# Feed-forward layers one slot sooner in a slot-scheduled post-norm transformer layer

## What is computed

```python
x = layernorm(x + attention(x))        # 16 query heads of width 16, 4 key/value heads
gate, up = split(x @ Wgu_q.T)          # weights made ternary in groups of 64
h = silu(gate) * up                    # 1024 wide
x = layernorm(x + rms_norm(h) @ Wproj_q.T)
```

## Time and profile before

| | |
|---|---|
| median of 3 runs | 559.68 us (559.02 to 562.63) |
| the profiled execution | 559.17 us |
| its span | 557.2 us |
| work outside the span (559.17 - 557.2) | 1.97 us |
| one element in the middle of the run | about 29.6 us |

### The profile page before, as it was taken

How to read it: one execution, slowest core, us unless ns; L and a number is a source line. 1 busy time by engine, 2 the same in 40 slices (tenths; PEclk the granted TensorE clock), 3 DMA queues, 4 the chain that set the end, 5 groups by cost and what they waited for, 6 DMA issues and landing times. The chain is left out here.

```text
span 557.2 us, 13565 instructions
## 1 busy us (share of the span) xinstructions
PE 521.8 (94%) x4152; PEld 444.7 (80%) x4152; DVE 443.0 (80%) x1009; ACT 363.6 (65%) x735; POOL 332.5 (60%) x511
## 2 busy tenths in 40 slices
PE   4687999999999999999999999999999999999884
PEld 4677778788888888888888888888888888776773
DVE  6877796868888887878797878888898888875784
ACT  4553774657576767676777767676777676767553
POOL 4566774245665756575756656656657565656744
PEclk9896999999999999999999999999999999999997
DMA  9777173616253636354454536162627162010001
GB/s 233 133 153 121 45 138 74 115 58 115 51 107 57 131 55 135 69 124 79 106 98 95 105 83 117 65 119 57 121 41 164 16 152 51 22 41 1 19 21 38
DMA packets 83395, 49.16 MB, mean 88 GB/s; under 512 B 39696, under 2 KB 83344, under 8 KB 83344
## 3 DMA queue, kind: packets, MB, share of 16 engines
q1 hardware_dynamic: 81456, 47.87, 41.7%
q10 hardware_dynamic: 1888, 0.66, 0.5%
HBM read 33.29 MB, written 14.68 MB: 86 GB/s over the span
## 5 line engine op out<-in xcount | busy, mean ns | idle before, releaser
L867 DVE TENSOR_REDUCE row_max<-short_ps 128x2 f32<-128x512 f32 x256 | 169.8, 681 | 37.1 <-PE short_ps L579 35.7
L1055 POOL TENSOR_TENSOR h_lo<-h_f,h_hi 128x256 fp32r<-128x256 f32 x116 | 85.5, 737 | 163.9 <-ACT h_hi L766 163.7
L794 ACT ACTIVATE probs<-exp_ps 128x1024 f32<-128x1024 f32 x128 | 130.8, 1022 | 41.7 <-PE exp_ps L588 41.3
L579 PE MATMUL short_ps<-k_st,q_st 65*128 65x256 f32 x512 | 108.5, 296 | 3.8 <-DVE row_max L867 3.4
L775 ACT ACTIVATE tanh<-ffn_ps 128x256 f32<-128x256 f32 x120 | 45.9, 383 | 89.3 <-PE ffn_ps L607 89.3
L579 PEld LDWEIGHTS short_ps<-k_st,q_st 65*128 65x128 f32 x512 | 88.3, 193 | 15.2 <-issue 2.5
L1060 POOL TENSOR_TENSOR sq_sum<-sq_sum,h_sq 128x256 f32<-128x256 f32 x111 | 83.1, 749 | 7.0 <-ACT h_sq L830 6.7
L588 PE MATMUL exp_ps<-q_st,k_st 67*128 67x512 f32 x256 | 81.5, 400 | 3.4 <-DMA q_st<-shift_lo 3.2
L607 PE MATMUL ffn_ps<-x1T_hi,wguT 128*128 128x256 f32 x480 | 80.0, 289 | 3.7 <-DVE h_f L953 3.5
L620 PE MATMUL down_ps<-wpT,h_hi 128*128 128x256 f32 x256 | 79.4, 332 | 3.9 <-DVE h_lo L856 2.9
L607 PE MATMUL ffn_ps<-x1T_lo,wguT 128*128 128x256 f32 x480 | 77.9, 285 | 0.0
(11 more groups left out here) (110 smaller groups left out, 834.5 us busy)
## 6 DMA issues: line engine op xcount, KB each, us to landing
q_st<-q_dram SPq DMA_DIRECT2D x128, 128.0 KB, 3.9
q_dram<-q_p SPq DMA_DIRECT2D x16, 512.0 KB, 3.0
k_st<-k_dram SPq DMA_DIRECT2D x64, 64.0 KB, 2.4
res<-in_L_attn_x_dram SPq DMA_DIRECT2D x16, 256.0 KB, 2.8
xn<-in_L_attn_x_dram SPq DMA_DIRECT2D x62, 64.0 KB, 2.8
out_dram<-y_out SPq DMA_DIRECT2D x15, 256.0 KB, 2.9
wgu_raw<-in_L_ffn_w_gate_up_dram SPq DMA_DIRECT2D x8, 256.0 KB, 6.1
k_dram<-k_p SPq DMA_DIRECT2D x16, 128.0 KB, 2.5
```

Source lines behind the costliest of these rows:

```text
L579: last = pe.matmul(bank[:, t * S:(t + 1) * S], q_st[0:PAD, st.par, head, t * P:(t + 1) * P], k_st[0:PAD, st.par, st.s % 4, :], start=True, ...
L794: act.activation(probs[:, st.s % 4], exp_ps[:], ACT.Exp).then_inc(exp_done, 1)
L867: dve.tensor_reduce(row_max[:, st.par, head * TT:(head + 1) * TT], short(n, f"max{i}")[:].rearrange("p (t k) -> p t k", t=TT), AX.X, ALU.m ...
L1055: pool.tensor_tensor(h_p[1][:, st.s % 4, :], h_f[:, st.s % 2, :], h_p[0][:, st.s % 4, :].bitcast(F32), ALU.subtract).then_inc(h_lo, 1)
```

## The change

Nine offsets of the chain behind the attention fall by one: `LN1_APPLY`, `X1_T`, `X1_HIGH`, `X1_LOW`, `FFN0` with all its chunk steps, `DOWN0`, `Y_COPY`, and the sum of squares with its mean and root. The offsets of the output projection (26), `O_ADD` (26), `RSTD1` (27), `LN2_STATS` (42), `RSTD2`, `LN2_APPLY` and `STORE` stay. On POOL the four operations of `RSTD1` now stand ahead of the slot's `h_lo`. The banks of `sq`, `x1` and `shift0` change with the slots that they now fall in.

```diff
-LN1_APPLY = 28
-X1_T = 29
-FFN0 = 31
+LN1_APPLY = 27
+X1_T = 28
+FFN0 = 30
...
-BANK_TABLE = {0: {"max0": 2, "max1": 0, "sq": 1},
+BANK_TABLE = {0: {"max0": 2, "max1": 0},
...
-              4: {"max0": 0, "max1": 2, "k": 1},
-              5: {"max0": 2, "max1": 1, "shift0": 0, "x1": 2},
+              4: {"max0": 0, "max1": 2, "k": 1, "x1": 0},
+              5: {"max0": 2, "max1": 1, "shift0": 2},
...
-              7: {"max0": 2, "max1": 0, "v": 1}}
+              7: {"max0": 2, "max1": 0, "sq": 2, "v": 1}}
...
                         normalised(pool)
+                if st := n.once(RSTD1):
+                    wait(pool, var1_done, st.count(TT, TT))
...
                 if st := n.chunk(H_LOW0):
...
-                if st := n.once(RSTD1):
-                    wait(pool, var1_done, st.count(TT, TT))
...
```

More of the change, by code:

```diff
@@ L48 @@
 PROJ_O = 26
-LN1_APPLY = 28
-X1_T = 29
-FFN0 = 31
-DOWN0 = 33
-Y_COPY = 40
+LN1_APPLY = 27
+X1_T = 28
+FFN0 = 30
+DOWN0 = 32
+Y_COPY = 39
 TWO_BANKS = SLOTS * (B - 1) + EXP0 + SLOTS
-SUM_SQ = 40
+SUM_SQ = 39
 LN2_STATS = 42
@@ L65 @@
 RSTD1 = 27
[L66 to L73, removed]
+X1_HIGH = 28
+X1_LOW = 29
+GATE0 = 30
+H0 = 30
+H_HIGH0 = 31
+H_LOW0 = 31
+MEAN_SQ = 39
+INV = 39
 RSTD2 = 44
@@ L1050, in slot @@
                         normalised(pool)
+                if st := n.once(RSTD1):
+                    wait(pool, var1_done, st.count(TT, TT))
+                    pool.tensor_tensor(ve1[:], mv1[:, :, 1], ln_eps[:], ALU.add).then_inc(ve1_done, 1)
+                    wait(pool, ve1_done, st.count(1, 1))
+                    rsqrt(rstd1[:], ve1[:], rstd1_done)
+                    wait(pool, rstd1_done, st.count(1, 1))
+                    pool.tensor_tensor(mean1[:], mv1[:, :, 0], minus_one[:], ALU.mult).then_inc(mean1_done, 1)
+                    wait(pool, mean1_done, st.count(1, 1))
+                    pool.tensor_tensor(shift1[:], mean1[:], rstd1[:], ALU.mult).then_inc(shift1_done, 1)
                 if st := n.chunk(H_LOW0):
```

## The result

The changed kernel took 573.91 us (median of 4 runs, 573.10 to 575.31) against 559.70 for the kernel before (4 runs too). The ratio is 1.0246, interval 1.0205 to 1.0288: slower. The profiled execution took 575.31 us, its span is 573.5 (before: 557.2), 16.3 longer.

What follows compares the result with a forecast made beforehand. PE's own list was taken to set the 29.6 us element. Middle 0.56 x 13 = 7.3, head 1.5, tail 0: 8.8 us on 559.17 gives 568.0, plus 0.5 for the median: 568.5 us, range 563.5 to 572.5.

Steps and rivals of the forecast that it cites:

- Rival (a): PE's busy time hides slack, so the middle costs nothing and head and tail nearly cancel: 559.7 to 562; chance 0.16.
- Term 1: Slot 6: PE's low half newly waits for DVE's x1T_lo, 0.57 us an element (0.54 to 0.59).
- Term 2: Slot 7: the old wait for x1T_lo goes, giving back 0.09 us an element (0.06 to 0.13).
- Term 3: Slot 0: without the sum of squares, PE waits for h_f, 0.1 us an element on average (0 to 0.3).
- Number of elements: Middle of the run: the cost per element counts 13 times, for elements 1 to 13.
- Term 4: Head: slot 30 gets gate/up products that are not hidden, +1.5 us (0.8 to 2.0).
- Term 5: Tail: one slot fewer, but the last x1 is late and a tanh held back; 0 us (-1.5 to +1).
- The covers: Moved roots, x1, ms, bank users and the copy of down_ps are ready before their readers, so they cost nothing.

Runs made afterwards that it cites:

- low_first: Changed kernel with DVE's x1_low ahead of shift_rows in slot 5, so x1T_lo no longer waits for the turn of the maxima; 564.98 us, ratio 1.0087.
- low_later: Changed kernel with x1_low moved behind slot 5's second maximum, so the wait for x1T_lo gets longer; 580.37 us, ratio 1.0350.
- again: The changed kernel run once more without an edit; 570.63 us, ratio 1.0194.
- both: Changed kernel with the edits of low_first and sq_back together; 560.76 us, ratio 1.0002.
- sq_back: Changed kernel with only the sum of squares, its mean and root put back in slot 0; 569.67 us, ratio 1.0165.
- roots_back: Changed kernel with RSTD1's roots on POOL again behind h_lo and the sum of squares; 596.86 us, ratio 1.0644.
- roots_only: Kernel before the change with only RSTD1's four POOL operations moved ahead of the slot's h_lo; 562.34 us, ratio 1.0032.
- both_bout: Kernel of both, with ADD_BOUT (sum of residual and bias, POOL) in slot 7 instead of slot 0; 560.08 us, ratio 0.9992.

## Why the prediction was right and where it was wrong

**Direction and mechanism: right, and shown.** PE's list sets the period, and the new wait for `x1T_lo` is the largest loss: `low_first` takes it away and with it 0.65 of the 0.86. Rival (a), no difference, is dead: `low_later` shows that a longer wait comes back in the element one to one (0.593 for 0.60). The Trainium skill ("Perfetto Trace Analysis", "Identifying the Most-Contended Engine") advises to judge how close PE is to its roofline by weight load time and not by matmul busy time. By it there were 15% to spare here (25.55 of 29.99 us). That is room for a better list; it did not take up a new wait in this one, which came back in full.

**The size: wrong.** The forecast was 8.8 us and the range ended at 572.5; the first measurement gave 14.2 more (573.91 against 559.70), `again` 9.6 (570.63 against 561.02). The 570.63 lies inside the range, but by a start that happened to be early: the element missed in both. Behind the start, which is chance, the two profiles of the changed kernel are 13.2 and 12.9 us longer than that of the kernel before (16.3 - 3.1 and 568.7 - 557.2 + 1.4). By its own terms:

- **Term 1 (0.57): failed in one clause.** "After the wait, the chain low half, tanh, `gated`, `h_f`, next gate sets slot 6 as it did, so nothing is won back there." The wait itself is 0.53 on average, inside the bounds. But the chain is longer than it was: PE's first group after a stop takes 0.10 more, and `tanh` and `h_f` are as much later. 0.53 + 0.11 = 0.64; `low_first` gives 0.65. The prediction's own rows had it: the groups at 102.16 and 308.67, both behind a stop, are listed with 0.74, the one at 289.52 with 0.64.
- **Term 2 (-0.09): size right, place half wrong.** I had high to low half in slot 7 at 0.48; it is 0.56, since that high half itself comes out of the wait for `h_f` and is slow. 0.02 came back there, and 0.08 behind the low half, which no longer starts from a stop (3.35 to 3.27 in `both`).
- **Term 3 (0.08): failed, measured 0.30.** (Its text says 0.1, the sum used 0.08.) `sq_back` gives 0.25, since there slots 2 and 3 got longer by 0.07; the table from before to after gives -0.21, +0.05, +0.02 in slots 0 to 2 and +0.44 in slot 7 without term 2's 0.10, together 0.30. "The 0.37 itself only moves" is wrong by 0.07: the sum of squares holds PE for 0.47 behind other products, 0.44 net. Slot 0 lost another 0.07 to 0.08 (2.13 where 2.34 - 0.37 = 1.97 was possible, so 0.16, of which I had 0.08): the hand-over of 0.05 was read in the loop, and outside it, in half of the elements, it is 0.15. And the high half in slot 1 is slow by 0.07 to 0.08, after a stop that I had priced at 0.05 and that the view of waits doesn't even list.
- **What I had not in the sum:** the turn of `x1` ends slot 4 instead of slot 5, which changes slots 4, 5 and 6 by +0.32, -0.28 and, without the wait, -0.06: nothing in all (-0.02). 0.64 - 0.10 + 0.30 - 0.02 = 0.82, against 0.83 by the table and 0.86 by the exponentials.
- **Number of elements: 13 was right.** Twelve of them give 10.32 where I had 6.7, and most of the thirteenth lies in slots 133 to 142.
- **Term 4 (head, +1.5): right.** +1.63. `shift_lo` ended 0.91 behind the turn there, and `x1T_lo` started 0.83 behind it.
- **Term 5 (end, 0, from -1.5 to +1.0): inside its bounds.** +0.60 from slot 142 on. The last `x1` turn stood 17.41 us behind the last exponential and stands 17.17 behind it now, so 0.24 of the at most 0.8 was won; the rest went ahead of it, and 0.83 was lost behind it. The wait there was to be longer than 1.02; it is 0.98. Ahead of the turn PE stood for 2.75 in three other listed stops (0.68 for the exponential's bank at 528.23, 1.08 and 0.99 for `h_lo` at 535.06 and 542.56), before for 1.45. Behind it, to the last down product, 22.40 passed instead of 21.57, with two stops that the kernel before lacks: 0.72 for `h_lo` at 554.12 and 0.61 ahead of the last sums at 565.36. No experiment took one of them away, so the account of the end is read from the trace alone.
- **The covers held in the middle.** No wait for `ms`, the copy or the roots appears, and `roots_back` shows what it would cost if one did.

PE's first projections and the clock of the first 60 us differ between executions by more than half of my forecast. I had set nothing aside for it: the range was made of the terms' bounds alone. Nor were those carried through: an element's upper end by them is 0.59 - 0.06 + 0.30 = 0.83 and not 0.75, which would have put the end of the range at 573.5 and not 572.5. That is still short of 573.91.

So of the 0.30 by which an element was missed, 0.19 is one omission, made in slots 6 and 1: a stop of PE was priced by the time at which it starts again, and not by how slowly it does. The 0.07 of the sum of squares in slot 7 is of the same kind, a first weight load without a lead.

## What to carry to other kernels

Where PE's list sets the period, price a new stop at its length plus about 0.1 us for the slower first group behind it, however short the stop is, and look also at the work behind the wait that is a chain. Take the length from where PE would have gone on, not from the bracket in the view of waits, which was 0.16 short here. Moving a step behind other products can cost the same 0.1 with no stop at all; the start of the first weight load against the first product shows it. Read hand-overs both inside and outside a hardware loop. Compare elements, not launches: means over a repeated period resolve 0.02 us, while the start alone moves a total by 4.5 us. Before a step is moved, look at what its consumers stand behind on their engine: one DVE operation in another place (`x1_low` ahead of the shift rows) was worth 0.65 us an element here, 5.7 us in the medians (570.63 to 564.98).

## What the runs showed of the hardware

- After a stop of PE of 0.42 us, of 1.02 us, or of one too short to be listed as a wait, the first group of four matmuls took 0.71 to 0.74 us instead of 0.64, at full granted clock. Its first weight load started with its first matmul and not 0.12 us ahead of it. Directly behind 128x128 turns, without a stop, the group took 0.72 and the lead was 0.02.
- The same four one-column matmuls held PE for 0.37 us behind score products and for 0.47 us behind the products with V, whether turns (128x128) or down products followed.
- From the end of DVE's `h_f` to the first matmul that waited for it, 0.05 us passed in the hardware loop and 0.15 us outside it in slot 0 of the changed kernel; why was not tried.
- Two executions of one program reached slot 15 at 49.48 and 53.96 us; the granted clock from 40 to 60 us was 0.91 and 0.74, the first weights were there at 7.92 and 8.88 us.
- Four of the ten profiled executions (`low_first`, `roots_only`, `roots_back`, `both_bout`) show a fall of the granted clock from 2.4 to 1.2 GHz near the end, behind waits of PE. In `roots_only` the five microseconds before had PE busy for 2.84; but the changed kernel, with waits of 0.99 and 0.98 us there, kept its clock. What decides it stays open. In `low_first`, whose program from slot 136 on is that of the changed kernel, the end took 1.4 us more with the fall in it (45.92 against 44.54).
